# Layer 0's attentions on one Trainium2 core: two chunks of both heads per unit, row maxima turned by VectorE and passed through DRAM

## The reference

```python
def _attn(xq, xc, Wq, Wk, Wv, Wo, bo):
    q = (xq @ Wq).reshape(B, N, HEADS, D_HEAD)
    k = (xc @ Wk).reshape(B, S, HEADS, D_HEAD)
    v = (xc @ Wv).reshape(B, S, HEADS, D_HEAD)
    scores = jnp.einsum('bnhd,bshd->bhns', q, k) * D_HEAD ** (-0.5)
    attn = jax.nn.softmax(scores, axis=-1)
    return jnp.einsum('bhns,bshd->bnhd', attn, v).reshape(B, N, HEADS * D_HEAD) @ Wo + bo

x = _attn(_ln(x, g1, b1), _ln(x, g1, b1), Wq1, Wk1, Wv1, Wo1, bo1) + x
x = _attn(_ln(x, g2, b2), context, Wq2, Wk2, Wv2, Wo2, bo2) + x
x = _geglu_ff(_ln(x, g3, b3), Wp, bp, Wf, bf) + x
```

## Time and profile before

| what | us |
|---|---|
| median of 3 runs | 3969.08 (3967.0 to 3972.28) |
| the profiled execution | 3972.02 |
| its span in the trace | 3970.2 |
| a0, from the start of its first loads to its last store | about 197 to 621 |
| a1, the same | about 1027 to 2197 |
| busy: PE / DVE / ACT / POOL | 3472.6 / 2430.1 / 2003.7 / 1125.2 |

### The profile page before, as it was taken

How to read it: one execution, slowest core, us unless ns; L and a number is a source line. 1 busy time by engine, 2 the same in 40 slices (tenths; PEclk the granted TensorE clock), 3 DMA queues, 4 the chain that set the end, 5 groups by cost and what they waited for, 6 DMA issues and landing times. The chain is left out here.

```text
span 3970.2 us, 57943 instructions
## 1 busy us (share of the span) xinstructions
PE 3472.6 (87%) x17596; PEld 2019.0 (51%) x17596; DVE 2430.1 (61%) x4148; ACT 2003.7 (50%) x3541; POOL 1125.2 (28%) x539
## 2 busy tenths in 40 slices
PE   7899995999799999999999588588488599999776
PEld 5644443888455555555554456333366444444254
DVE  4368884443477777777776344386254399999333
ACT  4356662445355555555555223167344168888633
POOL 0056660000366667766667000012000000000000
PEclk8999997999799999999999799789799789999888
DMA  6787766999855555555552432234454522222121
GB/s 213 270 187 194 194 161 247 332 318 312 217 134 134 124 125 132 134 139 122 123 130 57 151 111 96 80 113 133 147 193 139 148 77 87 95 95 100 58 85 42
DMA packets 363425, 590.63 MB, mean 149 GB/s; under 512 B 43675, under 2 KB 196859, under 8 KB 362151
## 3 DMA queue, kind: packets, MB, share of 16 engines
q1 hardware_dynamic: 362312, 586.05, 51.0%
q10 hardware_dynamic: 958, 2.62, 0.4%
HBM read 345.71 MB, written 239.97 MB: 148 GB/s over the span
## 5 line engine op out<-in xcount | busy, mean ns | idle before, releaser
L1198 DVE TENSOR_REDUCE a_blk_max<-a_mx 128x1 f32<-128x402 f32 (+1 forms) x1280 | 734.0, 587 | 430.5 <-PE a_mx L1001 411.5
L1148 ACT ACTIVATE a_prob<-a_sc 128x512 f32<-128x512 f32 (+1 forms) x1088 | 640.1, 597 | 505.1 <-PE a_sc L1030 470.2
L1569 ACT ACTIVATE a_prob<-a_sc 128x512 f32<-128x512 f32 (+1 forms) x1088 | 585.9, 598 | 136.6 <-PE a_sc L1492 131.0
L977 POOL TENSOR_TENSOR a_prob_sum<-a_prob,a_prob_sum 128x1024 f32<-128x1024 f32 x256 | 617.7, 2414 | 62.8 <-ACT a_prob L1148 53.7
L1041 PE MATMUL a_pv<-a_prob,a_v 128*64 128x512 f32 (+1 forms) x2176 | 585.9, 617 | 0.0
L1596 DVE TENSOR_REDUCE a_blk_max<-a_mx 128x1 f32<-128x402 f32 x1024 | 512.1, 568 | 73.6 <-PE a_mx L1479 69.4
L1001 PE MATMUL a_mx<-a_k_stack,a_q_stack 128*128 128x402 f32 (+1 forms) x1280 | 485.0, 389 | 38.2 <-DMA a_q_stack<-q_hi_cross 23.5
L1029 PE MATMUL a_sc<-a_q_stack,a_k_stack 128*128 128x512 f32 (+1 forms) x1088 | 460.5, 423 | 2.1 <-ACT a_q_second L1131 2.1
L1030 PE MATMUL a_sc<-a_q_second,a_k_second 65*128 65x512 f32 (+1 forms) x1088 | 432.1, 397 | 0.0
L977 POOL TENSOR_TENSOR a_prob_sum<-a_prob 128x1024 f32<-128x1024 f32 x128 | 312.1, 2448 | 417.8 <-ACT a_prob L1148 417.8
L1001 PEld LDWEIGHTS a_mx<-a_k_stack,a_q_stack 128*128 128x128 f32 x1280 | 247.8, 194 | 291.7 <-DVE a_blk_max L1198 109.6
(11 more groups left out here) (248 smaller groups left out, 4911.3 us busy)
## 6 DMA issues: line engine op xcount, KB each, us to landing
a_v<-v_cross SPq DMA_DIRECT2D x48, 768.0 KB
a_k_stack<-k_hi_cross SPq DMA_DIRECT2D x32, 801.0 KB, 6.7
a_k_stack<-k_lo_cross SPq DMA_DIRECT2D x32, 801.0 KB, 9.8
a_k_second<-k_hi_cross SPq DMA_DIRECT2D x32, 801.0 KB
v_cross<-p_v_sb SPq DMA_DIRECT2D x48, 512.0 KB, 4.1
k_hi_cross<-p_split_hi SPq DMA_DIRECT2D x120, 200.0 KB, 3.3
k_lo_cross<-p_split_lo SPq DMA_DIRECT2D x120, 200.0 KB, 3.2
a_q_stack<-q_hi_self SPq DMA_DIRECT2D x64, 256.0 KB, 4.9
```

Source lines behind the costliest of these rows:

```text
L977: nc.gpsimd.tensor_tensor(prob_sum[:, h], prob_of(c, cp, h), other, ALU.add)\
L1148: nc.scalar.activation(prob_of(c, cp, h)[0:rows, k, :], sc[0:rows, (c * E + e) % SCB, :], ACT.Exp, scale=a.scale).then_inc(exp_done, 1)
L1198: nc.vector.reduce_max(blk_max[:, r, h, t, nb:nb + 1], mx[:, (c * NI + n) % MXB, 0:a.blk], AX.X)\
L1569: nc.scalar.activation(prob[0:keys, tau % RC, m, :], sc[0:keys, e % SCB, :], ACT.Exp, scale=a.scale).then_inc(exp_done, 1)
```

## The change

For SELF0 and CROSS0 `attend_phase` is replaced by `attend_wide`; a2 and a3 keep `attend_narrow`. What is computed stays the same, and so does the number of maxima, score, value and denominator matmuls.

- A unit w is now a pair of chunks of both heads: a group has NCP units (2, 7), T = 32 * NCP in all, written out without loops. On TensorE a unit is: up to four score pairs (L1310, L1311), maxima up to `cut(w)` (L1294), the values of unit w - 1, both chunks in one run (L1333), if due the denominators (L1319), and maxima up to `pairs_by(w)`. Maxima go in pairs, one item for each head.
- The row: VectorE collects the maxima in `row_max`, turns it (L1406, 128x32; in cross after a reduction of 128x8x4) and SP stores the row to DRAM and loads it back to row 64 of `q_second`; `k_second` has -1 there. The transposes on TensorE and ScalarE's copies are gone. On SP's queue, after the loads of group 0, the store and load of its maxima stand ahead of the loads of group 1.
- The denominators go to a bank of `a_mx`. VectorE turns the bank (L1424, 128x512), takes the reciprocal of 16 columns (L1426) and turns them back, broadcast (L1429), in place of ScalarE's copy and the four reciprocals.
- Places: DEN_AT = NCP + 2, DIVIDE_AT = NCP + 3, HIGH_AT = NCP + 4. VectorE does `last_sums`, `divide` (L1449) and `low_part` (L1454) at the end of a unit, behind its reductions (L1415). ScalarE does `raw_copy` (L1361) and `high_part` (L1367) at the start of a unit, ahead of its exponentials (L1391).
- Buffers: 3 score banks in both, 4 banks for maxima, none of its own for `aux`. Before the first scores stand 20 (self) and 46 (cross) items instead of 8 and 32.
- The two scratch tensors in DRAM for maxima and inverses have a new layout, and layer 1's DMAs to and from them follow.

The core of the diff:

```diff
-        self.maxima = [dram(f"maxima{n}", [P, 32], F32) for n in range(2)]
-        self.inverse = [dram(f"inverse{n}", [4, NQ], F32) for n in range(2)]
+        self.maxima = [dram(f"maxima{n}", [32, P], F32) for n in range(2)]
+        self.inverse = [dram(f"inverse{n}", [32, P], F32) for n in range(2)]
...
+    DEN_AT, DIVIDE_AT, HIGH_AT = NCP + 2, NCP + 3, NCP + 4
...
+    def pairs_by(w):
+
+        return min(NG * PAIRS, -(-PAIRS * (NCP + LEAD + w + 1) // NCP))
+
+    def cut(w):
+
+        return (pairs_by(w - 1) + pairs_by(w) + 1) // 2
+
+    def place(p):
+
+        return p + sum(cut(i * NCP + DEN_AT) <= p for i in range(NG))
+
+    def den_place(i):
+        return cut(i * NCP + DEN_AT) + i
...
+            for n in range(SLOTS - 1):
+                load_kq(n)
+                load_second(n)
+                load_v(n)
+                if n == 0:
+                    store_maxima(0)
+                    load_maxima(0)
...
+            def denominators(i):
+                n = 2 * den_place(i)
+                pe.wait_ge(merged, 2 * (i + 1))
+                pe.wait_ge(item_read, n - MXB + 1)
+                for h in range(2):
+                    last = nc.tensor.matmul(mx[64 * h:64 * h + 64, n % MXB, :], pr.ones[:, 0:64],
+                                            chunk_sum[:, i % CS, h, :], start=True, stop=True)
+                last.then_inc(den_done, 1)
...
+            def values(w):
+                i, cp = divmod(w, NCP)
+                for ch in a.pair(cp):
+                    if ch == 0:
+                        pe.wait_ge(v_loaded[i % SLOTS], 16 * NV * (i // SLOTS + 1))
+                        if i:
+                            pe.wait_ge(pv_copied, i)
+                    pe.wait_ge(exp_done, step_of(i, cp, ch % 2, 1) + 1)
+                    keys = a.chunk_rows(ch)
+                    for h in range(2):
+                        last = nc.tensor.matmul(pv[64 * h:64 * h + 64, :], v[i % SLOTS][0:keys, ch, 64 * h:64 * h + 64],
+                                                prob_of(w, h)[0:keys, ch % 2, :], start=(ch == 0), stop=(ch == NC - 1))
+                    last.then_inc(pv_done, 1)
...
+            maxima(0, pairs_by(-1))
+            for w in range(T):
+                for ch in a.pair(w % NCP):
+                    for h in range(2):
+                        scores(w, ch % 2, h)
+                maxima(pairs_by(w - 1), cut(w))
+                if w:
+                    values(w - 1)
+                sums_at(w)
+                maxima(cut(w), pairs_by(w))
+            values(T - 1)
...
+            def high_part(i):
+                act.wait_ge(divided, i + 1)
+                if i >= OS:
+                    act.wait_ge(o_stored[i % OS], 32 * (i // OS))
+                nc.scalar.copy(o_hi[:, i % OS, :], o_full[:, i % OS, :]).then_inc(o_hi_done, 1)
...
+            def prob_free(w, h):
+                i, cp = divmod(w, NCP)
+                act.wait_ge(pv_done, i * NC + min(NC, 2 * cp + 2))
+                one = (max(cp, 1), h)
+                if one in pool_sums:
+                    act.wait_ge(pool_sum, i * len(pool_sums) + pool_sums.index(one) + 1)
+                else:
+                    act.wait_ge(dve_sum, i * len(dve_sums) + dve_sums.index(one) + 1)
...
+            for w in range(T):
+                i, cp = divmod(w, NCP)
+                if cp == 1 and i:
+                    raw_copy(i - 1)
+                if w >= HIGH_AT and (w - HIGH_AT) % NCP == 0:
+                    high_part((w - HIGH_AT) // NCP)
+                for ch in a.pair(cp):
+                    keys = a.chunk_rows(ch)
+                    for h in range(2):
+                        if w >= RC and ch % 2 == 0:
+                            prob_free(w - RC, h)
+                        e = step_of(i, cp, ch % 2, h)
+                        act.wait_ge(st_done, e + 1)
+                        nc.scalar.activation(prob_of(w, h)[0:keys, ch % 2, :], sc[0:keys, e % SCB, :],
+                                             ACT.Exp, scale=a.scale).then_inc(exp_done, 1)
...
+            def invert(i):
...
+                n = 2 * den_place(i)
+                dve.wait_ge(den_done, i + 1)
+                nc.vector.transpose(den[:], mx[:, n % MXB, :]).then_inc(item_read, 2)
+                dve.wait_ge(item_read, n + 2)
+                nc.vector.reciprocal(inv_cols[:], den[:].rearrange("p (k i) -> p k i", i=32)[:, :, 0])\
+                    .then_inc(inverted, 1)
+                dve.wait_ge(inverted, i + 1)
+                nc.vector.transpose(inv[:], inv_cols[:].rearrange("p (k o) -> p k o", o=1).to_broadcast([P, 16, 32]))\
+                    .then_inc(inv_turned, 1)
...
+            def last_sums(i):
+                for n, (cp, h) in enumerate(dve_sums):
+                    rows = a.chunk_rows(2 * cp)
+                    dve.wait_ge(exp_done, step_of(i, cp, 0, h) + 1)
+                    dve.wait_ge(pool_sum, (i + 1) * len(pool_sums) - 2 + h + 1)
+                    nc.vector.tensor_tensor(prob_sum[0:rows, h, 0, :], prob_sum[0:rows, h, 0, :],
+                                            prob_of(i * NCP + cp, h)[0:rows, 0, :], ALU.add).then_inc(dve_sum, 1)
+                if i >= CS:
+                    dve.wait_ge(den_done, i - CS + 1)
+                for h in range(2):
+                    dve.wait_ge(dve_sum, 2 * i + h + 1)
+                    nc.vector.tensor_tensor(chunk_sum[:, i % CS, h, :], prob_sum[:, h, 0, :], prob_sum[:, h, 1, :],
+                                            ALU.add).then_inc(merged, 1)
...
+            def divide(i):
+                dve.wait_ge(pv_copied, i + 1)
+                dve.wait_ge(inv_turned, i + 1)
+                nc.vector.tensor_tensor(o_full[:, i % OS, :], o_full[:, i % OS, :], inv[:], ALU.mult)\
+                    .then_inc(divided, 1)
...
+            for w in range(T + HIGH_AT):
+                blocks(pairs_by(w - 1), cut(w))
+                late(invert, w, DEN_AT)
+                blocks(cut(w), pairs_by(w))
+                if dve_sums:
+                    late(last_sums, w, NCP + 1)
+                late(divide, w, DIVIDE_AT)
+                late(low_part, w, HIGH_AT)
```

676 lines of the change are left out of this document (232 added, 444 removed).

## The result

The changed kernel takes 4294.4 us (median of 4 runs, 4289.3 to 4296.4) against 3970.7 us: a ratio of 1.081, interval 1.080 to 1.083. Slower was forecast, at 4129 us with 4200 as the upper bound; the loss is 324 us where I had 160. The profiled execution has a span of 4294.3 us against 3970.2.

What follows compares the result with a forecast made beforehand. TensorE, busy throughout, was taken as the bound. Self +75 (stalls), +43 (clock), -8; cross +13, +32 (clock), -9; prologues +24, tails -6, layout -4: together +160, giving 4129 us, range 3960 to 4200.

Steps and rivals of the forecast that it cites:

- the chain: Fourth score pair waits for the first exponential, that for the high part, that for VectorE's division; self stall 4.34 us.
- E + 4.34: E is the start of a unit's scores on TensorE; the self division was forecast to end at E + 4.49.
- The lock between VectorE and GpSimd: A VectorE operation with two SBUF inputs, coming while a GpSimd add runs, ends 0.55 us after that add.
- The clock: Half clock for 3.4 us after TensorE's pauses: 1.6 us a self group, 1.1 a cross group (two in three).
- Rival E: Pauses bring half clock each time, and for a second stretch in self: 4244 us, chance 0.11.
- The clash in cross: Cross division meets a GpSimd add ending at E + 2.48, E being the scores' start; stall 2.34 us.
- TensorE's savings: Joined value runs and dropped transposes save 1.54 us a self group and 2.92 a cross group, 142 us at most.
- The prologues: Ahead of the first scores, more maxima and queued loads cost +16 us in a1 and about +8 in a0.
- The tails: The drain at the end of both attentions loses eight reciprocals: -6 us together.
- the layout of layer 1's scratch: New layout of layer 1's scratch tensors turns many small writes into few: -4 us, bounds 0 and -15.
- that cover: Maxima row through DRAM on SP's queue costs nothing, as it has most of a group's time; otherwise at least 1.5 us.
- Rival D: Division and high part are done before the fourth score pair's turn, so the savings show: 3840 us, chance 0.10.

Runs made afterwards that it cites:

- run 3: The changed kernel with 16 unread matmuls on TensorE in the pause ahead of the fourth score pair: 4156.5 us, ratio 1.049.
- run 10: The kernel of run 8 with VectorE's low part four units later in cross, ahead of last_sums, and the store one group later: 3885.9 us, ratio 0.979.
- run 12: The kernel of run 10 with four PSUM banks for scores and three for maxima, in both attentions: 3937.5 us, ratio 0.993.
- run 8: Run 1 plus reordered self loads on SyncE, GpSimd dividing, a fourth cross probability buffer, group 1's loads before the wait for group 0's maxima: 4178.8 us, 1.053.
- run 1: The changed kernel with ScalarE's high part behind the exponentials of its unit, not ahead: 4062.4 us, ratio 1.025.

## Why the prediction was right and wrong

**Right: the sign, the place and the chain.** The pause stands once a group ahead of the fourth score pair, ended by an exponential behind the high part behind the division. In self the whole working held: division at E + 4.34 for 4.49, pause 3.98 for 4.2, and the group without half clock 14.96 us for 14.97. That last agreement is partly luck: TensorE saves 0.15 us less than I had, and the pause is 0.2 us shorter. The sign that I gave beside it, "a self group of 15.0 us", leaves out the 1.6 us of clock that the sum has for the same group; with it it would have read 16.6. The lock between VectorE and GpSimd is as the prediction read it from the earlier trace rows; the 128x512 turn, bounded there and taken as 0.71, lasts 0.72.

**Wrong: the size of four terms of the sum, 324 us instead of 160.**

- *The clock, 75 us forecast, 138 measured (run 3).* This is the step that failed most. I had taken 3.4 us of half clock from the rows after pauses of 3.43 and 1.89 us, and "two in three" in cross. After the pauses of 3.8 to 4.0 us it lasts 6.8 us in all the inner groups but one, and so costs more than the upper bound of 1.7 us that I gave it. Rival E named it with too small a chance (0.11) and too high a price: 3.4 us a group in both stages, for 2.1 and 2.8, and in cross spread over two pauses, where all of it came from one.
- *The clash in cross, a pause of 3.81 us for 2.2.* The division meets an add that has just begun, not one half done. 1.6 us x 29 = 47 us. I chose a middle for a thing that repeats with the same phase in every group; what is left of an add can be anything from 0 to 2.4 us, and both ends should have been carried into the range. The premise had a wrong count too: GpSimd has ten adds a cross group, not twelve (five units of two heads), 24 us and not 29, and the earlier trace rows show it, 66.44 of 100 us. So adds do not fill the group; they stand in a train, and the division falls into it each time.
- *TensorE's savings.* 2.3 us a cross group, not 2.92, and 1.39 in most self groups (10.79 us), not 1.54, by run 10, where TensorE hardly waits. The score pairs stand together now, and the fourth waits 0.1 us a unit for the first exponential (run 12); seven units, 0.65 us. In cross that is 0.6 x 29 = 17 us; in self the shorter pause makes up for it. Six ordinary steps (1.41 us) and the exponential's chain were equal in my own working, and I counted that as no wait.
- *The prologues, 40 us for 24.* First scores come 20 us later after the start of a1 (forecast 16), and 20 in a0 (forecast 8): 16 us of the 40 are the loads behind the first store and load of maxima, as they come back in run 8; how the rest divides was not tried. The tails gave back about 1 us, not 6, the layout of layer 1's scratch nothing that shows, not 4.

63 + 47 + 17 + 16 + 5 + 4 = 152 of the 164 us that were missing; the other 12 are not accounted for.

The wait that comes next was not in the forecast at all: had the pause alone been removed, SyncE's queue in self and the train of adds in cross would have kept the kernel 2.5% slower than before (run 1). For SyncE's queue the prediction said "I cost that at nothing, since row and loads have most of a group's time"; that cover was the pause itself, since in the changed kernel SyncE waits for the row's store for 27.0 us in 300 and in run 1 for 110.7. Rival D's 3840 counts on the full savings of TensorE, which no run reached; it took six edits to come to 3886.

## What to carry to other kernels

Packing one engine's work into longer runs moves every dependent step to the edge of a unit; before counting the saved matmuls, follow the chain from the last result of one unit to the first buffer that the next unit needs, and compare it with the time of the work between them. A small in-order step that waits for a long chain (here a cast of 0.6 us) is better placed behind the work that feeds the busiest engine than ahead of it: that alone was worth 232 us here. And give GpSimd's train of adds a gap, by a wait if need be, wherever VectorE has a step with two SBUF inputs on a short path.
